# Another order for the split source blocks of a dense graph aggregation

## The chip, the cores and the metric

The kernel runs on one core of one Trainium2 chip. The metric is the device time of one execution in microseconds (us); lower is better.

## The reference

6250 nodes with 256 features and 200,000 edges `src -> dst`. One layer of a graph network, a linear attention over heads, and a mixture of experts:

```python
xn = _layernorm(x)
neigh = xn[dst]
w = sigmoid(relu(neigh @ W1 + b1) @ W2 + b2)
num = segment_sum(neigh * w, src)            # 6250 rows
den = segment_sum(w, src)
x = x + where(den > 0, num / max(den, 1e-12), 0) + mix(xn)
x = x + experts(_layernorm(x))               # 6 experts, the best 2 for each node
```

Only the sums over edges, `num` and `den`, touch what is changed. `dst` is drawn as the square of a uniform number times 6250, so that few nodes are the `dst` of many edges.

## The kernel before, in words

**Stages.** The edges are turned into keys and sorted on VectorE (up to about 440 us of the trace), with the layer norms, the gate and the attention on the other engines beside the sort. Then come 49 rounds of aggregation (about 496 to 1351 us), and then the experts (to the end).

**A round** makes the sums of one block of 128 target nodes (`src`). The gated rows `y` of all 49 source blocks (`dst`) lie in SBUF in two parts, high and low, of 258 columns. For each source block the kernel builds a 128x128 matrix of edge counts and multiplies `y` by it. An edge slot is 128 edges of one pair of blocks. Since the first `SPLIT` = 6 source blocks have more edges than a slot holds, each of them is split into two half blocks of 64 lanes with a slot each: 55 slots in a round, in 14 groups of four (`A_GROUP`), the last of three.

A group goes through these steps, and `k` counts the groups of a round:

- VectorE, `mark_group` (L1791, instruction at L1801): compares lane numbers with the edges' lanes and writes one-hot matrices in bf16, `hot_dst` and `hot_src`, two instructions of 128x512. It waits until the group two before has been built (`built`).
- TensorE, `build` (L1374, L1382): one matmul for each slot, 128 columns for a whole block and 64 for a half block, into one of two PSUM banks.
- ScalarE, `keep_tile` (L1133, L1138): copies the built matrices, 128 columns for each source block of the group, to one of two buffers of `a_ring`.
- TensorE, `aggregate` (L1387, L1400): for each source block of the group two matmuls of 258 columns, which sum in PSUM over the round. It waits for the copy (`a_ready`).

TensorE's order in a round is build 1, aggregate 0, build 2, aggregate 1, and so on to build 0 of the next round, aggregate 13. So a copy has to be finished within one aggregate and one build. At the start of a round ScalarE first copies the finished sums of the round before (`keep_sums`, L1142, L1146), for which it waits until aggregate 13 is done, and only then copies group 1. The sums stand in `turned` in even rounds and in `front` in odd ones. The other work of a node block (normalise, route, rank) is put between these steps in pieces by an order written out by hand (`LEAD`).

**Which slots make a group** is set by `place_of_slot` (L102). Before, the groups 0 to 5 have two half slots and two whole ones each: three source blocks, a copy of 384 columns and six matmuls in the aggregate. The groups 6 to 12 have four whole blocks (512 columns, eight matmuls), and group 13 has three. In this order the slots' numbers also are the thresholds by which edges are found: `slot_row`, `slot_no`, `limit` and `thr_bits`, made once at the start (L1609 to L1630) from three iota tables of GpSimd (L722 to L725). `slot_row` is used after the sort, in `count_heads` (L1736).

**GpSimd** in the rounds: `gather_window(q)` (L842) copies two indices (L844) and issues two indirect DMAs (L848) that fetch the sorted keys of the target blocks 2q and 2q+1; `over_spread(n)` (L853) makes one root; `list_tokens(n)` (L860) copies an id (L862) and issues two indirect DMAs (L866). One trip of its loop covers an even and an odd round. VectorE reads the window at the start of an even round (`find_edges`, L1762).

## Time and profile before

| | |
|---|---|
| time, median of 3 runs | 1732.89 us (1728.47 to 1734.03) |
| the profiled execution, its own time | 1728.47 us |
| its span in the trace | 1726.7 us |
| mean granted clock of TensorE | 0.925 |
| TensorE busy | 1428.3 us, 83% |
| VectorE busy | 1354.0 us, 78% |
| ScalarE busy | 811.1 us, 47% |
| GpSimd busy | 665.5 us, 39% |

The span is what the trace shows from the first to the last instruction; the time of the execution has 1.8 us around it. PE is TensorE's matmuls, PEld its weight loads, which lie beside the matmuls; DVE is VectorE, ACT ScalarE, POOL GpSimd. The end of a matmul in the trace is modelled, so that two of them overlap in the list; the starts are the better marks.

### The profile page before, as it was taken

The numbers are of one execution on the slowest core, as the hardware profiler recorded it, in microseconds if no ns is written. First come the engines' busy times: TensorE is split into PE (matmuls) and PEld (weight loads), VectorE is DVE, ScalarE is ACT, GpSimd is POOL, SyncE is SP. The second block draws the span as 40 slices with busy tenths as digits, with TensorE's granted clock in tenths as the row PEclk, the third lists the DMA queues.
The fourth block names the chain that finished last, engine by engine and source line by source line (L and its number), as shares of the span: only waits on it lengthen the run. The fifth ranks groups of instructions, "written<-read, shape, count | busy, mean of one in ns | idle before, by whom it ended". The sixth has DMA issues, their size and how long they took to land.

```text
span 1726.7 us, 40180 instructions
## 1 busy us (share of the span) xinstructions
PE 1428.3 (83%) x12059; PEld 1329.7 (77%) x12059; DVE 1354.0 (78%) x3945; ACT 811.1 (47%) x1983; POOL 665.5 (39%) x669
## 2 busy tenths in 40 slices
PE   0147878646559999999999999999999399999896
PEld 0136777535559999999999999999999399998786
DVE  8998879889958788878888888888887556666565
ACT  1114556336625455555555555555555155555453
POOL 1563565664411222222222222222222323338777
PEclk9767889767779999999999999999999699999998
DMA  7000000003334111111011101110111344433442
GB/s 187 11 1 1 1 1 1 1 18 122 119 105 122 45 41 39 43 41 44 34 49 37 49 34 49 37 48 34 46 40 46 129 135 144 130 102 108 123 129 73
DMA packets 68547, 108.68 MB, mean 63 GB/s; under 512 B 14306, under 2 KB 47849, under 8 KB 68231
## 3 DMA queue, kind: packets, MB, share of 16 engines
q1 hardware_dynamic: 50726, 57.78, 11.9%
q0 software_dynamic: 17760, 50.16, 8.3%
q8 instruction: 29, 0.48, 0.1%
q14 instruction: 32, 0.26, 0.1%
HBM read 52.41 MB, written 57.47 MB: 64 GB/s over the span
## 4 chain that ended last, share of the span: by engine, by line
PE 60%; issue 15%; DVE 11%; POOL 7%; DMA 3%; ACT 1%; SPq 1%; DVEq 1%; another core or an unknown queue 0%; POOLq 0%; ACTq 0%
PE turned L1400 17%; PE front L1400 17%; PE turned L1382 9%; DVE sort_mem L1704 7%; POOL acc_mem L781 6%; PE turned L1541 4%; PE front L1541 4%; PE front L1561 3%; PE front L1429 1%; PE front L1422 1%; PE turned L1534 1%; DMA gath_mem<-in_dst 1%; DVE sort_mem L1801 1%; DVE sort_mem L1712 1%; ACT a_ring L1138 1%
## 5 line engine op out<-in xcount | busy, mean ns | idle before, releaser
L1801 DVE TENSOR_TENSOR sort_mem<-lane_bf,sort_mem 128x512 bf16<-128x512 bf16 x1372 | 519.0, 420 | 145.6 <-PE turned L1382 131.6
L1138 ACT ACTIVATE a_ring<-turned 128x384 fp32r<-128x384 f32 (+1 forms) x686 | 373.4, 544 | 408.9 <-PE turned L1382 405.3
L1400 PE MATMUL turned<-y_all,a_ring 128*128 128x258 f32 x2450 | 387.1, 296 | 8.8 <-ACT a_ring L1138 8.8
L1400 PE MATMUL front<-y_all,a_ring 128*128 128x258 f32 x2352 | 377.4, 297 | 1.1 <-ACT a_ring L1138 1.1
L1704 DVE TENSOR_TENSOR sort_mem<-sort_mem 128x320 f32<-128x320 f32 (+2 forms) x568 | 325.6, 634 | 3.0
L1400 PEld LDWEIGHTS turned<-y_all,a_ring 128*128 128x128 f32 x2450 | 317.5, 190 | 12.9 <-issue 11.2
L1400 PEld LDWEIGHTS front<-y_all,a_ring 128*128 128x128 f32 x2352 | 306.1, 190 | 4.7 <-ACT a_ring L1138 1.4
L1382 PE MATMUL turned<-sort_mem 128*128 128x128 bf16 (+1 forms) x2695 | 259.6, 217 | 3.8 <-DVE sort_mem L1801 2.0
L1382 PEld LDWEIGHTS turned<-sort_mem 128*128 128x128 bf16 x2695 | 139.6, 98 | 40.3 <-DVE sort_mem L1801 9.2
L1339 PE MATMUL turned<-ident,sort_mem 128*128 128x128 f32 x286 | 57.8, 368 | 105.9 <-DVE sort_mem L1704 105.2
L855 POOL TENSOR_TENSOR feat_mem<-feat_mem,ln_eps 128x1 f32<-128x1 f32 x49 | 13.2, 270 | 337.7 <-DVE feat_mem L1865 337.7
L781 POOL TENSOR_TENSOR acc_mem<-acc_mem,gath_mem 128x16 f32<-128x16 f32 (+1 forms) x25 | 101.0, 4040 | 108.1 <-ACT acc_mem L1033 108.1
L2102 DVE COPY acc_mem<-feat_mem 128x1796 f32 x112 | 123.2, 1102 | 21.4 <-issue 21.4
L1339 PEld LDWEIGHTS turned<-ident,sort_mem 128*128 128x128 f32 x286 | 47.3, 193 | 113.5 <-DVE sort_mem L1704 112.4
L2110 DVE TENSOR_TENSOR base<-front,acc_mem 128x256 f32<-128x256 f32 x108 | 45.7, 423 | 107.2 <-PE front L1561 64.3
L866 POOL DMA_INDIRECT token_lists<-feat_mem,list_at x98 | 100.9, 1029 | 58.0 <-POOL feat_mem L862 41.3
L1541 PE MATMUL front<-sort_mem,acc_mem 128*128 128x128 f32 x864 | 115.3, 276 | 4.1 <-ACT sort_mem L1221 3.3
L1541 PE MATMUL turned<-sort_mem,acc_mem 128*128 128x128 f32 x864 | 116.5, 278 | 1.1 <-DVE acc_mem L2102 1.1
L1561 PE MATMUL front<-acc_mem,sort_mem 128*128 128x256 f32 x432 | 111.7, 381 | 2.9 <-ACT sort_mem L1221 2.9
L1541 PEld LDWEIGHTS front<-sort_mem,acc_mem 128*128 128x128 f32 x864 | 105.4, 192 | 5.6 <-ACT sort_mem L1221 4.4
L1541 PEld LDWEIGHTS turned<-sort_mem,acc_mem 128*128 128x128 f32 x864 | 106.7, 194 | 2.1 <-ACT sort_mem L1215 1.1
L1221 ACT ACTIVATE sort_mem<-turned,acc_mem 128x128 f32<-128x128 f32 x216 | 67.5, 365 | 66.0 <-PE turned L1541 55.3
(250 smaller groups left out, 2120.5 us busy)
## 6 DMA issues: line engine op xcount, KB each, us to landing
base<-token_lists SPq DMA_DIRECT2D x54, 258.0 KB
base<-token_lists SPq DMA_DIRECT2D x54, 130.0 KB
gated_rows<-tab_mem SPq DMA_DIRECT2D x49, 128.5 KB, 3.1
late_mem<-mixed_rows SPq DMA_DIRECT2D x49, 128.0 KB
mixed_rows<-base SPq DMA_DIRECT2D x12, 512.0 KB
feat_mem<-in_L_ffn_expert_w SPq DMA_DIRECT2D x18, 256.0 KB, 5.6
base<-in_x SPq DMA_DIRECT2D x1, 3136.0 KB
base<-in_x SPq DMA_DIRECT2D x1, 2352.0 KB
```

Source lines behind the costliest of these rows:

```text
L781: nc.gpsimd.tensor_tensor(over_std[:, 0:heads], std_eps[:, 0:heads], minus_one[:, 0:heads], ALU.pow).then_inc(S["pool_step"], 1)
L866: nc.gpsimd.indirect_dma_start(out=token_lists, out_offset=bass.IndirectOffsetOnAxis(ap=list_at[slot][:, k:k + 1], axis=0), in_=token_row[ ...
L1138: nc.scalar.activation(a_ring[:, k % 2, :, :].rearrange("p s n -> p (s n)")[:, 0:width], ps_a[k % 2][:, 0:width], ACT.Copy).then_inc(S["a_ ...
L1221: nc.scalar.activation(to[:, s % 2, h * P:(h + 1) * P], ps[s % 2][:, h, :], ACT.Relu, bias=wts[:, s % PACK_SLOTS, bias_at + h:bias_at + h ...
L1339: last = nc.tensor.transpose(turned[:, at:at + P], held[:, at:at + P], ident[:, :])
L1382: last = nc.tensor.matmul(ps_a[k % 2][:, at:at + width], hot_dst[:, k % 2, n // 2, :, n % 2], hot_src[:, k % 2, n // 2, 0:width, n % 2], s ...
L1400: last = nc.tensor.matmul(ps_agg[odd], a_ring[:, k % 2, n, :], y_part(t, part), start=(t == 0 and part == 0), stop=(t == BLOCKS - 1 and pa ...
L1541: last = nc.tensor.matmul(ps[s % 2][:, o, :], wts[:, s % PACK_SLOTS, first:first + P], moving[:, s % 2, h * P:(h + 1) * P], start=(h == 0) ...
L1561: last = nc.tensor.matmul(ps_out[s % 2], hid_2[:, s % 2, h * P:(h + 1) * P], wts[:, s % PACK_SLOTS, at:at + DIM], start=(h == 0), stop=(h ...
L1704: nc.vector.tensor_tensor(outs[t], lower, upper, ops[t]).then_inc(sorted_half[half], 1)
L1801: nc.vector.tensor_tensor(hot[:, k % 2, 0:pairs, :, :], lane_bf[:, :, :].unsqueeze(1).broadcast_to([P, pairs, P, 2]), edges.unsqueeze(2).b ...
L2102: nc.vector.tensor_copy(wts[:, s % PACK_SLOTS, :], flat_packs[:, bass.ds(at, PACK)]).then_inc(S["wts_ready"], 1)
```

## The change

`place_of_slot` gives another order: the twelve half slots come first and fill the groups 0, 1 and 2 (two source blocks each, a copy of 256 columns and four matmuls in the aggregate), and the groups 3 to 12 have four whole blocks, group 13 three. All the rest follows from `place_of_slot` or goes with it:

- in the groups 0 to 2 the comparison for `hot_src` is made for the 64 lanes in use alone;
- the three iotas of `slot_row` are gone, and five small instructions of VectorE make it just before the sort; the instructions for `slot_no`, `limit` and `thr_bits` are others;
- in GpSimd's loop, `gather_window` goes ahead of the second `over_spread`, directly behind the first `list_tokens`.

```diff
 def place_of_slot(s):
-    group, at = divmod(s, A_GROUP)
-    if group >= SPLIT:
-        return s - SPLIT, 0, P
-    if at < 2:
-        return group, P // 2 * at, P // 2
-    return SPLIT + 2 * group + at - 2, 0, P
+    if s < 2 * SPLIT:
+        return s // 2, P // 2 * (s % 2), P // 2
+    return s - SPLIT, 0, P
...
-            for rows, steps, first in ((half_rows, [[2, SPLIT], [1, 2]], 0), (whole_rows, [[4, SPLIT], [2, 2]], 2 * SPLIT),
-                                       (rest_rows, [[2, SLOT_ROWS - SPLIT * A_GROUP]], 2 * SPLIT * (A_GROUP - 1))):
-                nc.gpsimd.iota(rows, pattern=[[2 * SLOT_ROWS, 2]] + steps, base=first, channel_multiplier=0,
-                               allow_small_or_imprecise_dtypes=True).then_inc(S["consts"], 1)
...
             with nc.gpsimd.Fori(1, FULL // 2) as q:
                 over_spread(2 * q - 1)
                 list_tokens(2 * q - 2, 2 * q - 2, 0)
+                gather_window(q + 2)
                 over_spread(2 * q)
-                gather_window(q + 2)
                 list_tokens(2 * q - 1, 2 * q - 1, 1)
...
-            dve.wait_ge(S["consts"], N_CONSTS)
-            nc.vector.tensor_tensor(own_row, slot_row, ident[:, :], ALU.mult).then_inc(S["slot_step"], 1)
...
+            dve.wait_ge(S["consts"], N_CONSTS)
+            nc.vector.tensor_scalar(slot_row_1, lane[:, :], float(SLOT_ROWS), float(SLOT_ROWS), ALU.is_ge, ALU.mult).then_inc(S["slot_step"], 1)
+            dve.wait_ge(S["slot_step"], 11)
+            nc.vector.tensor_tensor(slot_row_2, lane[:, :], slot_row_1, ALU.subtract).then_inc(S["slot_step"], 1)
+            dve.wait_ge(S["slot_step"], 12)
+            nc.vector.tensor_scalar(slot_row, slot_row_2, -2.0 * SPLIT, 0.0, ALU.add, ALU.max).then_inc(S["slot_step"], 1)
+            dve.wait_ge(S["slot_step"], 13)
+            nc.vector.tensor_tensor(slot_row, slot_row, slot_row_2, ALU.add).then_inc(S["slot_step"], 1)
+            dve.wait_ge(S["slot_step"], 14)
+            nc.vector.scalar_tensor_tensor(slot_row, slot_row_1, 2.0, slot_row, ALU.mult, ALU.add).then_inc(S["slot_step"], 1)
+
             dve.wait_ge(S["key_step"], 16)
...
-                pairs = -(-len(slots_here) // 2)
+                pairs, width = -(-len(slots_here) // 2), place_of_slot(slots_here[0])[2]
                 dve.wait_ge(S["built"], g + 1)
-                for hot, at in ((hot_dst, P), (hot_src, 0)):
+                for hot, at, lanes in ((hot_dst, P, P), (hot_src, 0, width)):
                     at += of * SLOT_ROWS + slots_here[0]
                     edges = edge_tab[:, at:at + 2 * pairs].rearrange("p (s t) -> p s t", t=2)
-                    nc.vector.tensor_tensor(hot[:, k % 2, 0:pairs, :, :],
-                                            lane_bf[:, :, :].unsqueeze(1).broadcast_to([P, pairs, P, 2]),
-                                            edges.unsqueeze(2).broadcast_to([P, pairs, P, 2]), ALU.is_equal).then_inc(S["hot_ready"], 1)
+                    nc.vector.tensor_tensor(hot[:, k % 2, 0:pairs, 0:lanes, :],
+                                            lane_bf[:, 0:lanes, :].unsqueeze(1).broadcast_to([P, pairs, lanes, 2]),
+                                            edges.unsqueeze(2).broadcast_to([P, pairs, lanes, 2]), ALU.is_equal).then_inc(S["hot_ready"], 1)
```

## Rows read from the trace of the kernel before

**Rows 1.** The page, a costly group: busy us, mean ns of one | idle before, what ended it.

```profile
L1801 DVE TENSOR_TENSOR sort_mem<-lane_bf,sort_mem 128x512 bf16<-128x512 bf16 x1372 | 519.0, 420 | 145.6 <-PE turned L1382 131.6
```

**Rows 2.** Busy time by stage, the 49 rounds (us, then PE, PEld, DVE, ACT, POOL busy, PEclk).

```profile
496.00:1351.00 855.00, 842.88 (x8095) 796.55 (x8094) 688.73 (x2649) 437.98 (x997) 206.68 (x312) 1.00 0.14 47
```

**Rows 3.** Timeline, an odd round begins (start us, us, engine, line, what, idle before).

```profile
932.85 0.96 POOL L866 DMA_INDIRECT token_lists<-feat_mem,list_at  x1 [0.30 <-issue]
...
933.61 0.49 ACT L1138 ACTIVATE a_ring<-turned 128x384 fp32r<-128x384 f32 x1 [1.22 <-PE turned L1382]
...
933.92 0.35 PE L1382 MATMUL turned<-sort_mem 128*128 128x64 bf16 x4
...
934.15 0.98 PE L1400 MATMUL front<-y_all,a_ring 128*128 128x258 f32 x6
...
934.43 0.39 ACT L1146 ACTIVATE sort_mem<-turned 128x257 f32<-128x257 f32 x1 [0.33 <-PE turned L1400]
...
934.71 0.49 ACT L1138 ACTIVATE a_ring<-turned 128x384 fp32r<-128x384 f32 x1
...
934.98 0.35 PE L1382 MATMUL turned<-sort_mem 128*128 128x64 bf16 x4
...
935.25 0.98 PE L1400 MATMUL front<-y_all,a_ring 128*128 128x258 f32 x6
...
936.08 0.35 PE L1382 MATMUL turned<-sort_mem 128*128 128x64 bf16 x4
...
936.47 0.49 ACT L1138 ACTIVATE a_ring<-turned 128x384 fp32r<-128x384 f32 x1
```

**Rows 4.** Timeline, an even round begins.

```profile
949.83 0.98 POOL L866 DMA_INDIRECT token_lists<-feat_mem,list_at  x1 [0.30 <-issue]
...
950.13 0.35 PE L1382 MATMUL turned<-sort_mem 128*128 128x64 bf16 x4
...
951.21 0.49 ACT L1138 ACTIVATE a_ring<-turned 128x384 fp32r<-128x384 f32 x1 [1.64 <-PE turned L1382]
...
951.83 0.99 PE L1400 MATMUL turned<-y_all,a_ring 128*128 128x258 f32 x6 [0.38 <-ACT a_ring L1138]
...
952.01 0.49 ACT L1138 ACTIVATE a_ring<-turned 128x384 fp32r<-128x384 f32 x1
```

**Rows 5.** Timeline, the window gather in the middle of an odd round.

```profile
941.07 0.39 POOL L844 COPY key_now<-key_at 128x2 uint32 x1
...
942.76 0.40 PE L1382 MATMUL turned<-sort_mem 128*128 128x128 bf16 x4
...
942.97 1.20 PE L1400 MATMUL front<-y_all,a_ring 128*128 128x258 f32 x8
...
943.64 0.96 POOL L848 DMA_INDIRECT sort_mem<-kept_keys,key_now  x1 [0.30 <-issue]
...
944.01 0.40 PE L1382 MATMUL turned<-sort_mem 128*128 128x128 bf16 x4
...
945.13 0.60 ACT L1138 ACTIVATE a_ring<-turned 128x512 fp32r<-128x512 f32 x1 [1.33 <-PE turned L1382]
```

**Rows 6.** Groups by line and form, 700 to 1200 us (busy us, mean ns, idle before).

```profile
L1138 ACT ACTIVATE a_ring<-turned 128x512 fp32r<-128x512 f32 x200 | 119.6, 598 | 144.2 <-PE turned L1382 144.2
```

**Rows 7.** Timeline of VectorE, the same even round.

```profile
953.19 0.75 DVE L1801 TENSOR_TENSOR sort_mem<-lane_bf,sort_mem 128x512 bf16<-128x512 bf16 x2
...
956.96 0.75 DVE L1801 TENSOR_TENSOR sort_mem<-lane_bf,sort_mem 128x512 bf16<-128x512 bf16 x2
```

**Rows 8.** Timeline of TensorE, the same even round.

```profile
956.75 0.96 PE L1400 MATMUL turned<-y_all,a_ring 128*128 128x258 f32 x6
957.77 0.41 PE L1382 MATMUL turned<-sort_mem 128*128 128x128 bf16 x4
```

**Rows 9.** Timeline, VectorE before the edges have landed.

```profile
10.67 0.28 DVE L1621 TENSOR_TENSOR sort_mem<-sort_mem,ident 128x128 f32<-128x128 f32 x1
...
15.21 0.99 DVE L1635 TENSOR_SCALAR acc_mem<-gath_mem 125x1600 f32<-125x1600 int32 x1 [3.32 <-DMA gath_mem<-in_dst]
```

More of the change, by code:

```diff
@@ L289, in gps_layer @@
         slot_row = sort_mem[:, 2 * COLS:2 * COLS + P]
-        own_row = sort_mem[:, 2 * COLS + P:2 * COLS + 2 * P]
-        rows_of_window = slot_row.rearrange("p (w r) -> p w r", w=2)
-        split_rows = rows_of_window[:, :, 0:SPLIT * A_GROUP].rearrange("p w (g t) -> p w g t", t=A_GROUP)
-        half_rows, whole_rows = split_rows[:, :, :, 0:2], split_rows[:, :, :, 2:A_GROUP]
-        rest_rows = rows_of_window[:, :, SPLIT * A_GROUP:SLOT_ROWS]
+        slot_row_1, slot_row_2 = (sort_mem[:, 2 * COLS + k * P:2 * COLS + (k + 1) * P] for k in (1, 2))
         dense_at = [0]
@@ L406, in gps_layer @@
         thr_bits = sb("thr_bits", [P, WINDOWS], I32)
-        slot, whole, slot_no, limit = (sb(n, [P, 1], I32) for n in ("slot", "whole", "slot_no", "limit"))
-        slot_sum = sb("slot_sum", [P, 1])
+        slot, pair_bit, slot_no, limit = (sb(n, [P, 1], I32) for n in ("slot", "pair_bit", "slot_no", "limit"))
         key_at = sb("key_at", [P, KEY_PAIRS, 2], U32)
@@ L523, in gps_layer @@
         tails_listed = [sem(f"tails_listed{k}") for k in range(TOP)]
-        N_CONSTS = 24
+        N_CONSTS = 21
         SPREAD_LINKS = 1
@@ L1609, in _ @@
             nc.vector.tensor_scalar(slot[:, :], row_no[:, :], SLOT_ROWS - 1, None, ALU.bitwise_and).then_inc(S["slot_step"], 1)
-            nc.vector.tensor_scalar(limit[:, :], row_no[:, :], 2, 1, ALU.bitwise_and, ALU.logical_shift_right).then_inc(S["slot_step"], 1)
+            nc.vector.tensor_scalar(pair_bit[:, :], row_no[:, :], SLOT_ROWS, 1, ALU.bitwise_and, ALU.logical_shift_left).then_inc(S["slot_step"], 1)
             dve.wait_ge(S["slot_step"], 2)
-            nc.vector.tensor_scalar(whole[:, :], slot[:, :], float(SPLIT * A_GROUP), None, ALU.is_ge).then_inc(S["slot_step"], 1)
@@ L1613, in _ @@
-            dve.wait_ge(S["slot_step"], 3)
-            nc.vector.tensor_tensor(limit[:, :], limit[:, :], whole[:, :], ALU.bitwise_or).then_inc(S["slot_step"], 1)
+            nc.vector.tensor_scalar(slot_no[:, :], slot[:, :], -2.0 * SPLIT, 0.0, ALU.add, ALU.max).then_inc(S["slot_step"], 1)
+            nc.vector.tensor_scalar(limit[:, :], slot[:, :], 2.0 * SPLIT, 1.0, ALU.is_ge, ALU.add).then_inc(S["slot_step"], 1)
             dve.wait_ge(S["slot_step"], 4)
-            nc.vector.tensor_scalar(limit[:, :], limit[:, :], 1.0, None, ALU.add).then_inc(S["slot_step"], 1)
@@ L1617, in _ @@
-            dve.wait_ge(S["slot_step"], 5)
+            nc.vector.tensor_tensor(slot_no[:, :], slot_no[:, :], slot[:, :], ALU.add).then_inc(S["slot_step"], 1)
             nc.vector.tensor_scalar(limit[:, :], limit[:, :], DST_SHIFT - 1, KEY_BASE, ALU.logical_shift_left,
                                     ALU.bitwise_or).then_inc(S["slot_step"], 1)
-            dve.wait_ge(S["consts"], N_CONSTS)
-            nc.vector.tensor_tensor(own_row, slot_row, ident[:, :], ALU.mult).then_inc(S["slot_step"], 1)
+            dve.wait_ge(S["slot_step"], 6)
@@ L1744, in count_heads @@
                                         ALU.bitwise_and).then_inc(S["slot_step"], 1)
-                dve.wait_ge(S["slot_step"], 13)
+                dve.wait_ge(S["slot_step"], 17)
                 nc.vector.tensor_copy(head_fields, head_bits).then_inc(S["slot_step"], 1)
-                dve.wait_ge(S["slot_step"], 14)
+                dve.wait_ge(S["slot_step"], 18)
                 pair_of = head_fields[:, 0, :].unsqueeze(2).broadcast_to(pairs_grid)
```

7 lines of the change are left out of this document (3 added, 4 removed).

## The prediction, made before the changed kernel ran

> **What bounds the kernel now.** I read the page first. TensorE is the busiest engine of the table, and VectorE's marks at L1801 are followed by their own waits: VectorE stood idle 145.6 us before them, nearly all of it until TensorE had built a group [rows 1]. Then I read the busy time by stage: in the 49 rounds it is busy 842.88 of 855.00 us at a granted clock of 1.00, which is the level of 2.4 GHz, and VectorE 688.73 us [rows 2]. So a round lasts 855/49 = 17.4 us, and TensorE sets it. Work taken off VectorE is worth something only where TensorE waits for it, and a few tenths of a microsecond of new waiting in each round are worth more than they look. Therefore I read the timelines of two rounds in a row for such places.
>
> An odd round [rows 3]. Build 1 starts at 933.92, aggregate 0 at 934.15, build 2 at 934.98. Aggregate 1 could start behind build 2, which takes 0.16 (from the full build of 0.21 below, by columns: 384 of 512), so at 935.14. It starts at 935.25: copy 1 began at 934.71, behind the copy of the sums (934.43), and ended at 935.20. TensorE waits 0.11 us for ScalarE. Build 3 starts at 936.08 and copy 3 at 936.47: 0.39 us from the start of a build to its copy.
>
> An even round [rows 4]. Here build 0 starts at 950.13 and its copy only at 951.21, 1.08 us later, while GpSimd works on an indirect DMA. TensorE waits for copy 0 and starts aggregate 0 at 951.83, 0.13 us after the copy's end. Copy 1 starts at 952.01, again behind the sums.
>
> **The change, part by part: the price list.** An aggregate of four source blocks is 942.97 to 944.01 = 1.04 us, and a full build 942.76 to 942.97 = 0.21 us [rows 5]. One of three blocks after a wait is 935.25 to 936.08 = 0.83 us [rows 3]. So a block costs 0.26 and what a wait adds is some 0.05: two blocks cost 0.55 us after a wait. A build of four half slots has 256 of 512 columns: 0.11 us. A copy of 384 columns takes 0.49 [rows 3] and one of 512 takes 0.60 us [rows 6], so 0.11 for each block, and 0.38 us for 256; the 257 columns of the sums take 0.39 [rows 3].
>
> TensorE's matmuls are the same in number and columns: 12 half slots, 43 whole ones and 98 of 258 columns in a round, before and after. The change moves no work off it. What can change is the waiting.
>
> **The odd round after.** Copy 0 is 0.11 shorter, but TensorE now comes to aggregate 0 at about 934.05 and ends it at 934.05 + 0.55 = 934.60, build 2 at 934.71. Copy 1 starts at 934.71 as before, since the sums ahead of it wait for the aggregate of the old round; it ends at 935.09, and aggregate 1 starts at 935.14. To compare with before, take from its 935.25 the work that is not yet done after: one block (0.26) and the wider build (0.05) give 934.94. The new order is 0.20 us behind. The short group no longer covers ScalarE's two copies.
>
> Group 3 is the other place. From the start of build 3 to aggregate 3 it needs 0.39 (release), 0.60 (copy of 512) and 0.05 to 0.13 (start, both seen above): 1.04 to 1.12 us. TensorE has build 3, aggregate 2 and build 4 to do meanwhile: 0.21 + 0.55 + 0.21 = 0.97. A wait of 0.07 to 0.15, taken as 0.11 us. Before, a group of three needed 0.39 + 0.49 + 0.13 = 1.01 against 0.16 + 0.83 + 0.16 = 1.15: no wait. Odd round: +0.31 us.
>
> **The even round after.** Copy 0 is shorter: -0.11. Aggregate 0 runs from 951.72 to 952.27, build 2 to 952.38; copy 1 ends at 952.01 + 0.38 = 952.39 and aggregate 1 starts 0.05 to 0.13 later: +0.07. Group 3: +0.11. In return a wait for VectorE goes. Aggregate 5 starts at 956.75 and build 7 at 957.77 [rows 8]: 1.02 us for three blocks that take between 3 x 0.26 = 0.78 and 0.83, say 0.81, so 0.21 of waiting; the marks for it end at 956.96 + 0.75 = 957.71 [rows 7]. After, VectorE has one instruction of half the size between the release of build 0 and these marks, that of group 2. Two of 512 take 0.75 [rows 7] and one 0.42 [rows 1], so they follow each other at 0.33 us. Half of that, 0.17, is saved if all of it goes with the elements, nothing if none does; I take 0.14, near the former. The marks end at 957.57; TensorE comes to build 7 at 957.56 - 0.11 + 0.07 + 0.11 = 957.63 and no longer waits: 0.14 us earlier than before. VectorE's marks for build 4 end at 953.94 - 0.14 = 953.80 [rows 7], just when TensorE wants them; that wait, if any, lies beside the one for copy 3. Even round: -0.14 us.
>
> The Trainium skill (VectorE: DVE Perf Modes, the section on the TRN2 errata) speaks against counting half: an instruction that reads SBUF pays a fixed latency whatever its size, and its measured fixed term is about 150 cycles; as an estimate from that page, 256 elements at two in a cycle take 0.29 us, 0.13 less than the row's 0.42, and the even round would stay at -0.14. If a half instruction cost half of 0.42, the marks would end 0.21 earlier and the sum would not change either, since TensorE comes to build 7 later than both.
>
> **Sum of the rounds.** A pair of rounds costs +0.31 - 0.14 = +0.17 us, and there are 24 pairs behind round 0: +4.1 us. The bounds: with every start at 0.05 and aggregate 1 of the even round in time the pair gives 0.0; with starts at 0.13, twice 0.15 for group 3, nothing back at build 7 beyond the 0.14 and 0.15 more for the marks of build 4 it gives some +0.5, +12 us.
>
> **The start.** The instructions on slots that are removed or altered were free: VectorE idles 3.32 us for the edges after them [rows 9]. The five new ones come behind the edges, on the path of the sort. One of 128x128 takes 0.28 us [rows 9], each waits for the one before: 5 x 0.28 = 1.4; two or three may be shorter. +1.3 us (0.8 to 1.6). The three iotas taken from GpSimd were hidden behind the same landing.
>
> **The moved gather.** Its two issues now follow those of the token lists (932.85 + 0.96 = 933.81 [rows 3]). From the copy of the indices to the second issue are 943.64 - 941.07 = 2.57 us [rows 5], so the second issue is at about 936.4, in group 4 of the odd round, where it was in group 8. VectorE needs the window at the next even round, over 10 us later either way. What counts is a side effect. Build 9's copy starts 1.12 us after its build (944.01 to 945.13 [rows 5]), build 0's 1.08 [rows 4], and not 0.39: around the second indirect DMA of a pair, the news of a finished build arrives late, at 1.38 to 1.49 us after that issue began. After, this stretch ends at 937.8 to 937.9. By the steps above build 4 starts at about 936.4 and build 5 at 937.8. A group of four has 0.21 + 1.04 + 0.21 = 1.46 against 1.12, so 0.34 us of slack, and I price this at zero. I count the old place as free too: TensorE's 12 us without matmuls in 855 [rows 2] leave no room for a loss there in each pair.
>
> Total: 1728.5 + 4.1 + 1.3 = 1733.9 for the profiled execution. It was 4.4 us below the median of the three runs, so the forecast for the median is 1732.9 + 5.4 = 1738.3 us.
>
> **The rivals.**
>
> 1. *ScalarE is not the limit, VectorE's relief counts (faster).* If the copies of 256 columns arrived in time everywhere, the even round would keep -0.11 and -0.21 and the odd one its 0.11: -0.43 a pair, -10 us, +1.3: 1724. For it: VectorE is busy 688.73 us of the stage and there is a wait for it in every even round. Against: rows 3 have ScalarE two copies behind at the round's start with a longer aggregate to cover them. It decides if aggregate 1 follows build 2 with no gap. A weak form, with the odd loss at half, ends near 1729.
> 2. *The waits cancel (no change).* The pair sums to 0.0 as in the lower bound: 1734.
> 3. *The moved gather hits a short cover (much slower).* If the late news falls on build 3 or 4 with the full delay, copy 4 ends at 937.9 + 0.60 = 938.5, and aggregate 4, wanted at 938.0, starts 0.6 us late in each pair: +14 us on top of the forecast, 1753. For it: the builds of [rows 4, 5] were released late by 0.7. Against: the copy at 933.61 started 0.76 us after a second issue [rows 3], so builds are also released at that distance, which would be 937.2 and would serve build 4. It decides where build 4 is released: harmless up to 937.3.
>
> **How the numbers follow.** From no change this kernel's measurement can tell about 0.3%, 5.2 us: the bounds are 1727.7 and 1738.1. Chances: the forecast 0.45, the cancelling waits 0.25, the gather (in part or in full) 0.17, VectorE's relief 0.13. The forecast straddles the upper bound, two thirds of it above: slower 0.30 + 0.17 + 0.03 = 0.50, faster 0.12, same 0.38. The range leaves out the stronger half of the fast rival and the strongest part of the slow one, together under 0.2: 1728 to 1752.
>
> **What would show it.** In the changed kernel's timeline of an odd round, aggregate 1 should start 0.05 to 0.1 us behind the end of copy 1, with an idle time of some 0.4 us before it; aggregate 3 should start at a copy's end in both rounds. Build 7 of the even round should follow aggregate 5 with no gap. The waits of TensorE for ScalarE in the rounds should grow, those for L1801 shrink, and VectorE's idle time grow by about 3 x 0.14 us a round. The copies of groups 4 and 5 in odd rounds show whether the gather delays them. Before the sort five new instructions should take 1.3 us. The prediction is wrong if the rounds get shorter: then a cover that I priced as too short is long enough, or the late news at the start of the even rounds has moved.

## The result: 1772.6 us, 2.5% slower, and the profile after

The changed kernel takes 1772.58 us (median of 4 runs, 1764.68 to 1775.53) against 1731.01 us for the kernel before (4 runs, 1728.47 to 1734.03) on the same chip: ratio 1.0248, interval 1.0212 to 1.0285. The sign was forecast. The size, +41.6 us, was not: the forecast was +5.4, and the result lies 20 us above the end of the range.

In the kernel after, the marks are L1796 (before L1801), ScalarE's copy L1126 (L1138), the aggregate L1388 (L1400), the build L1370 (L1382), the copy of the sums L1134 (L1146), the window gather L832 and L836 (L844, L848) and the list L850 and L854 (L862, L866).

I read the page first (groups: out<-in, count | busy us, mean ns | idle before them and its releaser):

```profile
L1796 DVE TENSOR_TENSOR sort_mem<-lane_bf,sort_mem 128x512 bf16<-128x512 bf16 x1372 | 498.2, 406 | 207.2 <-PE turned L1370 189.9
L1126 ACT ACTIVATE a_ring<-turned 128x512 fp32r<-128x512 f32 (+2 forms) x686 | 370.9, 545 | 462.5 <-PE turned L1370 447.4
L1388 PE MATMUL front<-y_all,a_ring 128*128 128x258 f32 x2352 | 376.0, 297 | 37.6 <-ACT a_ring L1126 37.6
L1388 PE MATMUL turned<-y_all,a_ring 128*128 128x258 f32 x2450 | 387.2, 296 | 10.8 <-ACT a_ring L1126 10.8
```

VectorE's marks are 20.8 us cheaper than in [rows 1] (519.0), which is the 0.42 us a round that the prediction took, and VectorE waits 61.6 us longer. TensorE now waits 48.4 us for ScalarE's copies. The busy time by window says that the clock is at its full level here, as in [rows 2]:

```profile
500.00:1400.00 900.00, 847.69 (x8083) 800.15 (x8082) 672.09 (x2650) 435.01 (x999) 199.93 (x312) 1.00 0.13 45
```

Then the timeline, for the length of the rounds: from aggregate 1 of round 0 (aggregate 0 comes over 6 us ahead of it in both) to the last 14 matmuls. Before, then after:

```profile
502.38 0.96 PE L1400 MATMUL turned<-y_all,a_ring 128*128 128x258 f32 x6
...
1349.11 1.93 PE L1400 MATMUL turned<-y_all,a_ring 128*128 128x258 f32 x14
```

```profile
502.70 0.73 PE L1388 MATMUL turned<-y_all,a_ring 128*128 128x258 f32 x4
...
1395.09 1.94 PE L1388 MATMUL turned<-y_all,a_ring 128*128 128x258 f32 x14
```

So 846.73 us became 892.39: +45.7 us, +1.90 us for each of 24 pairs, and that is nearly all of the 47.4 us by which the two profiled executions differ (1775.93 and 1728.5). From here on "the rounds" means this length, read in one execution of each kernel; it is free of what varies ahead of round 0. Every execution read below took within 0.4% of its kernel's median, but for that of e6b (1894 us against 1737), which isn't read.

An odd round begins, kernel after (timeline):

```profile
955.06 0.96 POOL L854 DMA_INDIRECT token_lists<-feat_mem,list_at  x1 [0.30 <-issue]
...
955.18 0.29 PE L1370 MATMUL turned<-sort_mem 128*128 128x64 bf16 x4
...
956.54 0.38 ACT L1126 ACTIVATE a_ring<-turned 128x256 fp32r<-128x256 f32 x1 [1.93 <-PE turned L1370]
...
956.98 0.75 PE L1388 MATMUL front<-y_all,a_ring 128*128 128x258 f32 x4 [0.58 <-ACT a_ring L1126]
...
957.71 0.72 PE L1388 MATMUL front<-y_all,a_ring 128*128 128x258 f32 x4
...
958.27 0.41 PE L1370 MATMUL turned<-sort_mem 128*128 128x128 bf16 x4
958.34 0.96 POOL L836 DMA_INDIRECT sort_mem<-kept_keys,key_now  x1 [0.30 <-issue]
...
959.91 1.09 ACT L1126 ACTIVATE a_ring<-turned 128x512 fp32r<-128x512 f32 x2 [0.96 <-PE turned L1370]
...
960.56 1.23 PE L1388 MATMUL front<-y_all,a_ring 128*128 128x258 f32 x8 [1.11 <-ACT a_ring L1126]
```

Two places. Build 0 starts 0.12 us after the list's second issue, and its copy starts 1.36 us after the build, 1.48 after that issue. In [rows 3] the copy came 0.76 after the issue. Build 3 starts beside the gather's second issue (958.34), its copy comes 1.64 us after the build and 1.57 after the issue, and aggregate 3 waits 1.11 us. Undisturbed, 0.33 to 0.44 us lie between a build and its copy, by its width (in e5, below). VectorE's marks, which wait for the same builds, start at the same late moments (956.54, 959.91), so it isn't ScalarE that is late but the news that TensorE has finished. The even round has the first place only: issue 973.94, build 0 974.27, copy 975.43, aggregate 0 975.95 after a wait of 0.45 us.

The start is as priced: the halves of the edges begin at 28.48 us and the sort at 30.98, with five new instructions of 0.22 to 0.29 us between; before, 28.50 and 29.75. That is +1.25 us.

### The profile page after: what moved, and what is told of

Its sections match the earlier page's. It is cut to its first block, busy times and chain, and to the rows that moved or that the text cites. A ratio compares the mean times of both kernels' runs of the same rounds, so it can differ in the third digit from the quotient of the medians.

```text
span 1773.8 us, 40181 instructions
## 1 busy us (share of the span) xinstructions
PE 1438.8 (81%) x12059; PEld 1337.7 (75%) x12059; DVE 1339.3 (76%) x3949; ACT 806.8 (45%) x1983; POOL 655.2 (37%) x666
## 4 chain that ended last, share of the span: by engine, by line
PE 63%; issue 12%; DVE 12%; POOL 5%; DMA 3%; ACT 3%; DVEq 1%; another core or an unknown queue 1%; SPq 1%; POOLq 0%; ACTq 0%
PE turned L1388 18%; PE front L1388 16%; PE turned L1370 10%; DVE sort_mem L1688 8%; PE turned L1529 4%; PE front L1549 4%; PE front L1529 4%; POOL acc_mem L769 4%; ACT a_ring L1126 2%; PE turned L1522 1%; PE front L1417 1%; PE front L1410 1%; DVE sort_mem L1696 1%; DMA gath_mem<-in_dst 1%
## 5 line engine op out<-in xcount | busy, mean ns | idle before, releaser
L1796 DVE TENSOR_TENSOR sort_mem<-lane_bf,sort_mem 128x512 bf16<-128x512 bf16 x1372 | 498.2, 406 | 207.2 <-PE turned L1370 189.9
L1126 ACT ACTIVATE a_ring<-turned 128x512 fp32r<-128x512 f32 (+2 forms) x686 | 370.9, 545 | 462.5 <-PE turned L1370 447.4
L1388 PE MATMUL front<-y_all,a_ring 128*128 128x258 f32 x2352 | 376.0, 297 | 37.6 <-ACT a_ring L1126 37.6
L1388 PE MATMUL turned<-y_all,a_ring 128*128 128x258 f32 x2450 | 387.2, 296 | 10.8 <-ACT a_ring L1126 10.8
L1388 PEld LDWEIGHTS front<-y_all,a_ring 128*128 128x128 f32 x2352 | 305.9, 190 | 44.7 <-ACT a_ring L1126 44.4
L1388 PEld LDWEIGHTS turned<-y_all,a_ring 128*128 128x128 f32 x2450 | 317.4, 190 | 14.8 <-issue 11.6
L1370 PE MATMUL turned<-sort_mem 128*128 128x128 bf16 (+1 forms) x2695 | 258.7, 217 | 2.3 <-DVE sort_mem L1796 2.2
L1370 PEld LDWEIGHTS turned<-sort_mem 128*128 128x128 bf16 x2695 | 147.5, 98 | 36.8 <-DVE sort_mem L1796 3.1
L769 POOL TENSOR_TENSOR acc_mem<-acc_mem,gath_mem 128x16 f32<-128x16 f32 (+1 forms) x25 | 93.6, 3743 | 108.1 <-ACT acc_mem L1021 108.1
L850 POOL COPY feat_mem<-node_id 128x1 int32 (+1 forms) x49 | 8.9, 182 | 320.0 <-DVE list_at L1907 320.0
L854 POOL DMA_INDIRECT token_lists<-feat_mem,list_at x98 | 99.4, 1014 | 58.3 <-POOL feat_mem L850 41.5
```

The lines of the kernel that those rows point to most:

```text
L769: nc.gpsimd.tensor_tensor(over_std[:, 0:heads], std_eps[:, 0:heads], minus_one[:, 0:heads], ALU.pow).then_inc(S["pool_step"], 1)
L854: nc.gpsimd.indirect_dma_start(out=token_lists, out_offset=bass.IndirectOffsetOnAxis(ap=list_at[slot][:, k:k + 1], axis=0), in_=token_row[ ...
L1126: nc.scalar.activation(a_ring[:, k % 2, :, :].rearrange("p s n -> p (s n)")[:, 0:width], ps_a[k % 2][:, 0:width], ACT.Copy).then_inc(S["a_ ...
L1370: last = nc.tensor.matmul(ps_a[k % 2][:, at:at + width], hot_dst[:, k % 2, n // 2, :, n % 2], hot_src[:, k % 2, n // 2, 0:width, n % 2], s ...
L1388: last = nc.tensor.matmul(ps_agg[odd], a_ring[:, k % 2, n, :], y_part(t, part), start=(t == 0 and part == 0), stop=(t == BLOCKS - 1 and pa ...
L1796: nc.vector.tensor_tensor(hot[:, k % 2, 0:pairs, 0:lanes, :], lane_bf[:, 0:lanes, :].unsqueeze(1).broadcast_to([P, pairs, lanes, 2]), edge ...
```

## The experiments

Two theories stood against each other. A, late news: TensorE's signals reach the other engines up to 1.2 us late (1.64 us after a build's start and not 0.44) around the second of two indirect transfers that GpSimd issues close together, and the change brings builds of short groups under them. B, short covers: the short groups give ScalarE too little time, whatever GpSimd does. After the first runs a rival D stood beside A: any second transfer does it, at whatever distance.

All verdicts are ratios to the kernel before, run beside on the same chip; the last column is the length of the rounds in the profiled execution, read as above. The medians come from several chips, on which the kernel before took 1731.0 to 1739.6 us, so rows are to be compared by their ratios or by their rounds.

| kernel | median us | ratio, interval | rounds us |
|---|---|---|---|
| before | 1731.0 | 1 | 846.7 |
| after | 1772.6 | 1.0248, 1.0212 to 1.0285 | 892.4 |
| e1 order alone | 1756.9 | 1.010, 1.006 to 1.014 | 867.0 |
| e2 gather alone | 1758.9 | 1.012, 1.0086 to 1.0153 | 872.9 |
| e3 after, full marks | 1778.5 | 1.0215, 1.0178 to 1.0252 | 893.2 |
| e4 before, list earlier | 1711.7 | 0.9853, 0.9826 to 0.988 | 826.2 |
| e5 e1, list earlier | 1727.1 | 0.9949, 0.9926 to 0.9973 | 840.8 |
| e8 after, list earlier | 1756.9 | 1.0137, 1.0079 to 1.0195 | 864.4 |
| e7 after, one gather transfer | 1754.2 | 1.0106, 1.0062 to 1.015 | 864.0 |
| e6 after, no gather | 1753.3 | 1.0119, 1.0085 to 1.0154 | 864.2 |
| e9 before, gap in pairs | 1719.7 | 0.9887, 0.9839 to 0.9935 | 829.8 |
| e10 after, gap in pairs | 1740.3 | 0.9999, 0.9971 to 1.0027 | 845.1 |
| e6b before, no gather | 1737.2 | 0.9973, 0.9941 to 1.0004 | none |
| e12 e5, sums later | 1730.2 | 0.9944, 0.9928 to 0.996 | 836.6 |
| e13 e4, sums later | 1719.1 | 0.9878, 0.9837 to 0.9919 | 825.5 |

### e1 and e2: each half of the change alone

e1 is the kernel after with

```diff
-                gather_window(q + 2)
                 over_spread(2 * q)
+                gather_window(q + 2)
```

and e2 the kernel before with the reverse.

> The changed kernel with the gather put back to its old place, behind the second over_spread. Theory A (late news: around the second indirect DMA of a pair the news of finished builds is held back, and the moved gather puts this on group 3): the 1.3 us wait ahead of aggregate 3 in odd rounds goes, 24 times 1.1, so about 1745 us; if the 0.7 us ahead of aggregate 0 in odd rounds goes as well, 1728 to 1735. Theory B (short covers, as forecast: the copies of ScalarE are not covered by the short groups, wherever the gather stands): within 5 us of the changed kernel, 1768 to 1778.

> The old kernel with the gather moved alone. Theory A: the second issue comes at about 3 us into the odd round, build 3 or 4 is released 1 to 1.4 us late and the longer groups of the old order cover 0.2 to 0.5 of it: 0.7 to 1.2 us in each of 24 pairs, 1748 to 1760 us. Theory B: no change, 1726 to 1736.

The new order costs 20.2 us in the rounds and the moved gather 26.2. By the ratios e1 (1.006 to 1.014 times 1731 us is 1741 to 1755) meets A's first value of about 1745, e2 (1746 to 1757) meets A's range, and neither meets B's. Together the rounds cost 46.4 us, against 45.7 for the whole change, but the halves don't add place by place (the table of the distances, further down): aggregate 0 of odd rounds comes 0.64 us later in e1, 0.72 in e2, and 0.63 in the kernel after, once and not twice; aggregate 3 comes 0.53 us later in e2, but 1.09 later in the kernel after than in e1. That the two differences nearly cancel is luck. In e1 aggregate 0 of odd rounds waits as in the kernel after, with the gather far away, but aggregate 3 hardly does:

```profile
949.62 0.96 POOL L854 DMA_INDIRECT token_lists<-feat_mem,list_at  x1 [0.30 <-issue]
...
949.73 0.29 PE L1370 MATMUL turned<-sort_mem 128*128 128x64 bf16 x4
...
951.13 0.38 ACT L1126 ACTIVATE a_ring<-turned 128x256 fp32r<-128x256 f32 x1 [1.96 <-PE turned L1370]
...
951.57 0.75 PE L1388 MATMUL front<-y_all,a_ring 128*128 128x258 f32 x4 [0.61 <-ACT a_ring L1126]
```

In e2, on the old order, build 0 of the odd round (944.36) is just as late, though its group is not a short one and the gather's issues come only after it, and the gather's second issue (947.69) delays aggregate 3 too:

```profile
944.25 0.97 POOL L866 DMA_INDIRECT token_lists<-feat_mem,list_at  x1 [0.30 <-issue]
...
944.36 0.35 PE L1382 MATMUL turned<-sort_mem 128*128 128x64 bf16 x4
...
945.76 0.49 ACT L1138 ACTIVATE a_ring<-turned 128x384 fp32r<-128x384 f32 x1 [1.97 <-PE turned L1382]
...
946.31 0.99 PE L1400 MATMUL front<-y_all,a_ring 128*128 128x258 f32 x6 [0.63 <-ACT a_ring L1138]
...
949.67 0.98 PE L1400 MATMUL front<-y_all,a_ring 128*128 128x258 f32 x6 [0.24 <-ACT a_ring L1138]
```

B can't explain e2. It stays possible for a part of e1. Nor does A say why moving the gather makes the news at aggregate 0, ahead of it, late.

### e3: the narrower marks undone

```diff
-                pairs, width = -(-len(slots_here) // 2), place_of_slot(slots_here[0])[2]
+                pairs, width = -(-len(slots_here) // 2), P
```

> The changed kernel with the comparison for hot_src at its full 128 lanes in every group. If VectorE's marks matter anywhere in the changed kernel: slower by 0.14 us for each of 3 marks in 49 rounds where they are waited for, up to 20 us, so up to 1793. Theories A and B both: VectorE is waited for hardly anywhere, within 5 us of the changed kernel.

VectorE's marks rise from 498.2 to 517.4 us on the page, and the rounds by 0.8 us. The intervals of e3 and of the kernel after overlap. The relief of VectorE is worth nothing here.

### e4 and e5: the list's transfers two steps earlier

Both kernels, the old order and the new one (with the gather at its old place), with the place in the list worked out two steps, which is one group, earlier:

```diff
-            peak=28, exp=30, probs=37, top=40, top_exp=42, index=43, marks=44, share=46, rank=46, place=50)
+            peak=28, exp=30, probs=37, top=40, top_exp=42, index=43, marks=44, share=46, rank=46, place=48)
```

> The old kernel with the last piece of routing (place), and so the indirect DMAs of the token lists, one group earlier in the round. Theory A: the held stretch ends about 1.3 us earlier, before build 0 or right behind it, so the wait of 0.6 us for copy 0 at the start of even rounds goes or shrinks: 0.3 to 0.7 us in each pair, 1714 to 1724 us. Theory B: the wait there is for ScalarE's copy itself and does not depend on the DMA: 1726 to 1736.

> The new order of the groups with the gather at its old place, and the list's transfers issued two groups of the step earlier (lead of place 48 in place of 50), as in e4_place48_before on the old order. Theory A (late news: TensorE's signals reach the other engines late around the second of two indirect transfers on GpSimd, and the new order's short first groups stand under them): with the list's transfers moved away from the round's first groups nearly all of the 18 us that the new order cost in e1_order_alone goes, aggregate 0 of odd rounds waits under 0.1 us for its copy (0.61 in e1), and the time comes within 8 us of e4's 1711.7, so 1710 to 1720, ratio to the kernel before 0.984 to 0.991. Theory B (short covers: the short groups give their copies too little time, whatever GpSimd does): the waits at aggregate 0 stay near 0.4 to 0.6 us per round, and the time stays 15 us or more above e4, so 1727 or more, ratio 0.993 or more.

Both are faster than with place 50: e4 by 20.5 us in the rounds, e5 by 26.2 against e1. e4 beats both kernels of this case, and gains more than the 0.3 to 0.7 us a pair that A expected. In it TensorE waits for no copy at the start of a round; the second issue (936.47) lies ahead of build 13, and aggregate 0 follows build 1 at once:

```profile
938.60 0.96 PE L1400 MATMUL front<-y_all,a_ring 128*128 128x258 f32 x6
939.41 0.35 PE L1382 MATMUL turned<-sort_mem 128*128 128x64 bf16 x4
939.56 0.97 PE L1400 MATMUL turned<-y_all,a_ring 128*128 128x258 f32 x6
```

Build 13 starts 0.54 us after that issue, is copied 1.00 us after its start, and still aggregate 13 comes 1.22 us after aggregate 12, as in the other rounds: this is the longer cover at work. But most of these builds aren't released late at all. In the rounds 8 to 43 the copy of build 13 comes 0.38 us after it in 32 of 36 rounds of e4, and after 0.38 to 0.45 us in all 36 of e5, though the list's two issues are 1.32 to 1.49 us apart, as before. e5, an even round, where the second issue is 1.49 us behind the first:

```profile
938.88 0.97 POOL L854 DMA_INDIRECT token_lists<-feat_mem,list_at  x1 [0.30 <-issue]
...
939.41 0.34 PE L1370 MATMUL turned<-sort_mem 128*128 128x128 bf16 x3
...
939.79 0.49 ACT L1126 ACTIVATE a_ring<-turned 128x384 fp32r<-128x384 f32 x1 [0.34 <-PE turned L1388]
```

So a second transfer close behind the first isn't enough to make the news late; in e5 build 13 starts 0.35 us (odd rounds) and 0.53 us (even rounds) after it. What else it takes, these traces don't show.

The late news at the round's start costs 0.85 us a pair in the old order (20.5 / 24) and 1.09 in the new one (26.2 / 24). But e5 is 14.6 us over e4, above what A expected of it (within 8 us): 0.61 us a pair belong to the order by itself, as B had it. In e5's timeline aggregate 1 starts 0.05 us behind the end of its copy, which had to follow the copy of the sums (L1134), and aggregate 3 starts 0.05 us behind the end of copy 3:

```profile
959.22 0.73 PE L1388 MATMUL turned<-y_all,a_ring 128*128 128x258 f32 x4
...
959.38 0.39 ACT L1134 ACTIVATE sort_mem<-front 128x257 f32<-128x257 f32 x1 [0.51 <-PE front L1388]
...
959.66 0.38 ACT L1126 ACTIVATE a_ring<-turned 128x256 fp32r<-128x256 f32 x1
...
960.09 0.74 PE L1388 MATMUL turned<-y_all,a_ring 128*128 128x258 f32 x4
...
960.89 0.72 PE L1388 MATMUL turned<-y_all,a_ring 128*128 128x258 f32 x4
...
961.12 0.60 ACT L1126 ACTIVATE a_ring<-turned 128x512 fp32r<-128x512 f32 x1 [0.26 <-PE turned L1370]
...
961.77 1.22 PE L1388 MATMUL turned<-y_all,a_ring 128*128 128x258 f32 x8
```

These waits are short, and no idle time is printed for them. They show only in the distances of the aggregates: 0.87, 0.80 and 0.88 us for three groups of the same two blocks.

### e8: the whole change, list earlier

> The whole change with the list's transfers two groups earlier. Theory A: the wait at the round's first aggregate goes, the one at aggregate 3 of odd rounds (1.11 us in the kernel after, behind the window's gather) stays if the gather still starts beside groups 3 and 4, or moves with it one group earlier: GpSimd's queue has the gather right behind the first list, so its time depends on when GpSimd is through with it. Expected 1.0 us times 24 rounds above e5 if it stays: 1730 to 1745, ratio 0.995 to 1.003. Theory B: the short groups wait as before, 1760 or more.

The rounds are 23.7 us longer than in e5, 0.99 a pair for the moved gather again, though GpSimd comes to it one group earlier. The late stretch has moved with it from group 3 to group 2:

```profile
950.89 0.96 POOL L836 DMA_INDIRECT sort_mem<-kept_keys,key_now  x1 [0.30 <-issue]
...
951.00 0.29 PE L1370 MATMUL turned<-sort_mem 128*128 128x64 bf16 x4
...
952.54 0.38 ACT L1126 ACTIVATE a_ring<-turned 128x256 fp32r<-128x256 f32 x1 [1.25 <-PE turned L1370]
...
952.98 0.74 PE L1388 MATMUL front<-y_all,a_ring 128*128 128x258 f32 x4 [0.65 <-ACT a_ring L1126]
```

The build 0.11 us behind the second issue is copied 1.54 us later, in a group of 256 columns as in one of 512. The median is 12 us above the end of what A expected (1745): that range stood on e5's expected 1710 to 1720, and e5 took 1727. The step from e5 to e8, expected at 24 us, is 23.7 in the rounds.

### e7, e6 and e6b: one gather transfer, or none

e7 leaves out the second of the two indirect transfers of each window's gather in the loop, e6 and e6b both, in the kernel after and in the one before. They compute another list of edges so, and the flag that would send the kernel down another path (`cut_flag`) is forced to 0. The core of e7:

```diff
-                for half in range(2):
-                    nc.gpsimd.indirect_dma_start(
-                        out=window[:, half * P:(half + 1) * P], out_offset=None, in_=kept_keys,
-                        in_offset=bass.IndirectOffsetOnAxis(ap=key_now[:, half:half + 1], axis=0)).then_inc(S["window_in"], 16)
+                    nc.gpsimd.indirect_dma_start(
+                        out=window[:, 0:P], out_offset=None, in_=kept_keys,
+                        in_offset=bass.IndirectOffsetOnAxis(ap=key_now[:, 0:1], axis=0)).then_inc(S["window_in"], 16)
```

> The kernel after with only the first of the two indirect transfers of each window's gather inside the loop (window's second half isn't filled, the list of edges is so partly another, and the cut flag is forced to 0 so that the same path is run). Theory A (the second transfer of a pair is what holds TensorE's news): aggregate 3 of odd rounds waits under 0.4 us for its copy (1.11 us in the kernel after) and the time falls by about 1 us times 24, to 1745 to 1755. Rival C (any indirect transfer on GpSimd, or the copy ahead of it, does it): the wait at aggregate 3 stays over 0.8 us, and the time is within 8 us of the kernel after, 1765 to 1780. Theory B: as rival C.

> The kernel after without any of the indirect transfers of the window's gather inside the loop (later windows are stale, so the edges are partly others; the cut flag is forced to 0). Theory A: the wait at aggregate 3 of odd rounds goes to under 0.3 us and the time to 1742 to 1752; what is left over the kernel before is aggregate 0's wait behind the list's transfers. Theory B: the wait at aggregate 3 stays at 0.8 us or more, time 1765 to 1780.

> The kernel before without the indirect transfers of the window's gather inside the loop (later windows are stale, so the edges are partly others; the cut flag is forced to 0). The prediction took the gather's old place to be free. If so: 1729 to 1736, ratio 0.997 to 1.003. If the gather costs something at its old place too, as its move took 1.0 us a pair from the order alone: 1707 to 1722.

One transfer costs as little as none: 28.4 and 28.2 us less than the kernel after, in the rounds (e6's median is 1.3 us over what A expected). With the first transfer in place, build 3 (953.13) is copied as soon as ScalarE is free, and aggregate 3 starts at 954.36, without a wait of its own:

```profile
951.96 0.98 POOL L841 DMA_INDIRECT sort_mem<-kept_keys,key_now  x1 [0.82 <-POOL key_now L832]
...
953.13 0.41 PE L1375 MATMUL turned<-sort_mem 128*128 128x128 bf16 x4
...
953.72 1.25 ACT L1131 ACTIVATE a_ring<-turned 128x512 fp32r<-128x512 f32 x2
...
954.36 1.22 PE L1393 MATMUL front<-y_all,a_ring 128*128 128x258 f32 x8
```

So here it is the second transfer that holds the news, not the first and not the copy ahead of them. e6b's interval (0.9941 to 1.0004) includes 1: at its old place the gather was free, as the prediction had it, or cost 0.6% at most. Free doesn't mean that the news was on time there. In the kernel before, build 10 is copied 1.09 to 1.14 us after its start in 17 of 18 odd rounds (the prediction's rows show one, as build 9), but the aggregates 9, 10 and 11 follow each other at 1.26 and 1.71 us, as in e9 below, where build 10 is copied after 0.44 us.

### e9 and e10: a gap inside each pair

In both kernels one more copy of GpSimd's own, its wait and a nop stand between the two indirect transfers of every pair:

```diff
                 for k in range(TOP):
+                    if k:
+                        nc.gpsimd.tensor_copy(pad_list[:, :], node_id[:, 0:2]).then_inc(S["id_ready"], 1)
+                        pool.wait_ge(S["id_ready"], 2 * n + 2)
+                        pool.nop().then_inc(S["slot_free"], 1)
                     nc.gpsimd.indirect_dma_start(
```

> The kernel before with one small copy of its own, its wait and a nop put on GpSimd between the two indirect transfers of every pair (list and gather), so that the second begins some 1.0 us later than now, about 2.3 us after the first and not 1.3. Theory A in the form 'two transfers close behind each other hold TensorE's news': the late copies at the even round's start go (1.08 us from build 0 to its copy in the kernel before), and the time falls towards that of e4_place48_before, to 1712 to 1720, ratio 0.987 to 0.993. Rival D: any second indirect transfer of a pair holds the news however late it comes; then the hold only moves by 1 us, copy 1 or 2 becomes the late one, and the time stays within 10 us of before, 1725 to 1740. Theory B: no change but for GpSimd's own time, 1728 to 1738.

> The same gap in the kernel after. Theory A (close pairs): all three late places go, and what is left is the short covers as in e5_place48_order, so 1727 to 1737, ratio 0.995 to 1.002 (the kernel after had 1.0248). Rival D: the holds move by 1 us for the lists and by 1 to 2 us for the gather; 1755 to 1780. Theory B: 1765 to 1780.

The kernel before loses 17.0 us of its rounds, and the one after 47.3, so much that it is level with the kernel before. e10, an even round begins:

```profile
952.86 1.08 POOL L865 DMA_INDIRECT token_lists<-feat_mem,list_at  x1 [0.86 <-POOL feat_mem L856]
...
955.03 1.14 POOL L865 DMA_INDIRECT token_lists<-feat_mem,list_at  x1 [0.85 <-POOL pad_list L862]
...
955.50 0.29 PE L1381 MATMUL turned<-sort_mem 128*128 128x64 bf16 x4
...
955.62 0.73 PE L1399 MATMUL turned<-y_all,a_ring 128*128 128x258 f32 x4
...
955.78 0.39 ACT L1145 ACTIVATE sort_mem<-front 128x257 f32<-128x257 f32 x1 [0.50 <-PE front L1399]
...
956.07 0.38 ACT L1137 ACTIVATE a_ring<-turned 128x256 fp32r<-128x256 f32 x1
```

The issues are 2.17 us apart (955.03 - 952.86), not 1.35 as in the kernel after (955.06 - 953.71). 0.75 us behind the second one the sums' copy starts, 0.16 us behind the start of aggregate 0, the same distance as in e5 (959.22 and 959.38), and copy 1 follows it directly. Rival D wanted these late. In the rounds 8 to 43 the builds that start 0.31 to 0.46 us after the list's second issue are copied 0.33 us later in 35 of 35 rounds. By the ratio, the time of e10 is what A with close pairs gave (0.995 to 1.002). The gap also shifts the second issue by some 0.8 us against the builds, and e5 shows that place alone can make a close pair harmless. Against luck of place speak that it happens at all three places of the kernel after at once, that the kernel before gains as well, and that e7's lone transfer, 1.98 us behind the list's second (951.96 - 949.98), held nothing either. So the gap takes the late news away, but whether by the distance or by the shift that comes with it isn't shown. No distance between 1.51 and 1.98 us was tried.

### e12 and e13: one of ScalarE's two copies out of the way

What is left of the new order's price in e5? Here the copy of the sums is put behind the copy of group 1, on e5 and, as a control, on e4:

```diff
-                    if j == 0 and (not isinstance(i, int) or i):
-                        keep_sums(i, odd, not isinstance(i, int) or i > 1)
                     if j % 2 == 0 and not (last and j // 2 + 1 == A_GROUPS):
                         keep_tile(i, j // 2 + 1)
+                    if j == 0 and (not isinstance(i, int) or i):
+                        keep_sums(i, odd, not isinstance(i, int) or i > 1)
```

> e5_place48_order with ScalarE's copy of the finished sums put behind the copy of group 1 and not ahead of it, at the start of each round. Theory B' (what is left of the new order's price, 15 us in e5 over e4, is ScalarE's copies under short groups): in e5's trace aggregate 1 starts 0.05 us behind the end of its copy, and that copy starts behind the sums'; with the two exchanged the copy is 0.28 us earlier and the aggregate follows the one before it 0.14 us earlier, in each of 48 rounds: -7 us, 1716 to 1723, ratio to the kernel before 0.988 to 0.993 (e5 0.9949). If the remaining price lies elsewhere (VectorE's marks, TensorE's own starts), the time stays within 3 us of e5.

> e4_place48_before with the same exchange. In its trace aggregate 1 follows aggregate 0 without a gap, so all theories expect no change here: ratio to the kernel before 0.983 to 0.988 (e4 0.9853). It is the control of the exchange and the candidate for the fastest version.

The ratio doesn't tell e12 from e5, and misses what B' expected (0.988 to 0.993). The rounds are 4.2 us shorter, not 7, and 0.7 in the control. Aggregate 1 now follows aggregate 0 after 0.72 us (e5: 0.87), but where ScalarE has other work, in one round of each pair, a part comes back at group 3:

```profile
944.81 0.73 PE L1388 MATMUL front<-y_all,a_ring 128*128 128x258 f32 x4
...
945.53 0.74 PE L1388 MATMUL front<-y_all,a_ring 128*128 128x258 f32 x4
...
946.32 0.74 PE L1388 MATMUL front<-y_all,a_ring 128*128 128x258 f32 x4
946.36 0.41 ACT L1140 ACTIVATE sort_mem<-sort_mem 128x256 f32<-128x256 int32 x1
...
946.66 1.28 ACT L1126 ACTIVATE a_ring<-turned 128x512 fp32r<-128x512 f32 x2
...
947.30 1.22 PE L1388 MATMUL front<-y_all,a_ring 128*128 128x258 f32 x8
```

Copy 3 stands behind another activation (L1140) and aggregate 3 comes 0.98 us after aggregate 2, where e5 has 0.88. So the wait at group 1 was what B said, and ScalarE's queue takes a third of the gain back two groups on.

## Why the prediction was right in its direction and wrong in its size

All of it in one table: the distance from aggregate to aggregate, in us, worked out from their starts in the timeline, each the median of 18 rounds between 8 and 43. "13 to 0" is from the last aggregate of the round ahead to the first of this one.

| kernel | even 13 to odd 0 | odd 0 to 1, 1 to 2, 2 to 3, 3 to 4 | odd 13 to even 0 | even 0 to 1, 1 to 2, 2 to 3 | pair of rounds |
|---|---|---|---|---|---|
| before | 1.04 | 1.10, 0.99, 0.96, 0.96 | 1.55 | 0.99, 0.97, 0.96 | 34.72 |
| e4 | 0.96 | 0.96, 0.98, 0.96, 0.96 | 0.96 | 0.96, 0.98, 0.96 | 33.83 |
| e5 | 0.93 | 0.86, 0.80, 0.88, 1.28 | 0.93 | 0.87, 0.80, 0.88 | 34.42 |
| e1 | 1.68 | 0.72, 0.78, 1.01, 1.28 | 1.52 | 0.73, 0.80, 0.88 | 35.57 |
| e2 | 1.76 | 0.99, 0.96, 1.49, 0.99 | 1.59 | 0.98, 0.97, 0.96 | 35.89 |
| after | 1.67 | 0.72, 0.78, 2.10, 1.28 | 1.54 | 0.72, 0.80, 0.88 | 36.68 |

A pair of the kernel after is 1.96 us longer than one before: 1.09 at aggregate 3 of the odd round (2.10 against e1's 1.01), 0.63 at its aggregate 0, and 0.24 for all the rest. The sum of the rounds had +0.17 for that rest and nothing for the two others. That 0.24 is near 0.17 is partly luck, as the parts below show.

- **The step that failed most: "I price this at zero", of the moved gather.** It costs 25.4 us in the kernel after (892.4 - 867.0): 1.06 us a pair. (e2's 26.2 us are not its price alone: 0.72 us of its pair's 1.17 stand at aggregate 0, and 0.53 at aggregate 3.) The reasoning placed the late stretch on builds 4 and 5, whose groups of four blocks have 0.34 us of slack. Even there zero didn't follow: a stretch that ends at 937.8 releases build 4, started at 936.4, 1.4 us after its start and not 0.39: late by three times the slack. Only the early release at 0.76 made it free. It fell on build 3, whose cover is a short group, and aggregate 3 comes 2.10 us after aggregate 2 instead of 1.01. Two errors of place did that. The second issue came 3.28 us after the list's (958.34 - 955.06), I had 3.55. And build 3 came 3.21 us after it (958.27 - 955.06), where my steps have 2.84 (935.14 + 0.55 - 932.85): aggregate 0 was 0.72 us late, and the way to aggregate 1 shorter by 0.36 us. The slow rival was the right mechanism, at 0.6 us a pair where it measured 1.1.
- **The odd round's aggregate 0 was never in the sum.** I took copy 0 to be released when it had been (933.61). It is released 1.48 us after the issue, not 0.76, in the kernel after, and 1.51 in e1; 13 to 0 goes from 1.04 to 1.68 there. e2 shows the same on the old order, so short groups aren't needed for it. The release at 0.76 was no stray sample: in the kernel before the copy comes 0.61 to 0.68 us after build 0 in 17 of 18 odd rounds. In the kernel after it comes 1.34 to 1.40 us after it in 18 of 18, in e1 in 17 of 18 (1.32 to 1.40) and in e2 in 18 of 18 (1.35 to 1.41). The build stands at the same distance from the issue in all of them (0.10 and 0.11 us), and why the news got through in the one and not in the others stays open.
- **The short covers, +0.31 us in the odd round, hold, but only where no late news hides them.** In e5 group 1 costs 0.15 (0.87 - 0.72), group 3 some 0.10 (0.88 - 0.80 and 1.28 - 1.26), in both rounds: 0.5 us of the 0.61 a pair that e5 has over e4; e12 shows the part at group 1, the part at group 3 is read from the distances alone. In e1 and in the kernel after group 1 costs nothing, since copy 0 itself is late and copy 1 ready by then: 0.72.
- **The even round, -0.14 us, was wrong in e5's setting and partly right in the kernel after.** Its aggregates 5 and 6 follow each other without a gap as forecast (1.26 to 1.27 us for four blocks). But 13 to 0 there stayed at 1.54 (1.55 before), so the 0.11 for the shorter copy 0 was not had.
- **The lists' late news stood in the sum as a constant of both kernels.** It isn't one: 0.85 us a pair before, 1.09 in the new order (e4, e5).
- **"TensorE's 12 us without matmuls leave no room for a loss" was no bound.** e4 took 20.5 us out of the rounds. There TensorE counts as busy 836.5 of 848.6 us in the kernel before and 826.4 of 827.5 in e4, for the same matmuls: part of the waiting is counted as busy.
- **Right:** VectorE's marks (-0.42 us a round) and that the relief is worth next to nothing (e3); the start (+1.25 for +1.3); the gather's old place as free (e6b), within its interval; the waits that grew (TensorE for ScalarE) and shrank. VectorE's relief as a rival is out.

The Trainium skill (VectorE: DVE Perf Modes, the section on the TRN2 errata) had half-size marks dearer than half; the trace agrees: one of 256 elements takes 285 ns against 421 for 512, in the groups by form of the kernel after. The estimate worked out from that page was 0.29 us.

## What to carry to other kernels

When a queue of DMA issues is moved past other work, look up in the trace what the other engines saw around each issue, at every place where it occurs, and take the worst as the price unless it is known why another is better. A harmless place of the kernel before is no promise: build 0's copy came 0.61 to 0.68 us after it in 17 of 18 odd rounds there, and over 1.3 us in 18 of 18 after the change. Place such issues where a late release is covered: in the kernel before build 10's copy is late in 17 of 18 odd rounds and no distance of aggregates shows it. Here two steps earlier gave 1.5% on the kernel before (e4), and one small instruction between two indirect transfers 1.1% (e9). And check each "slack" with all the shifts that the change itself makes: two errors of place, of 0.27 and 0.37 us, made one of 1 us.

## What the runs showed of the hardware that was not expected

News of TensorE's finished builds reaches ScalarE and VectorE late at several places where it falls beside the second of two indirect transfers that GpSimd issues some 1.35 us apart. In the kernel after a copy starts 1.36 us (build 0) and 1.64 us (build 3) after the build's start instead of 0.33 to 0.44, and 1.44 to 1.61 us after the issue. It is gone with one transfer instead of two (e7), and with a small copy between the two, which puts them 2.17 us apart (e10). A close pair isn't enough: in e5 the list's issues are 1.32 and 1.49 us apart, and build 13, 0.35 and 0.53 us behind the second, is copied in time in 36 of 36 rounds. What holds the news, and why some places are released in time in nearly every round and others in hardly any, the traces don't show.
